# One core, three graph layers: VectorE's small work dealt out to GpSimd and ScalarE, its order changed, and score rows brought by DMA

## What is computed

```python
si = x @ attn_w[l, :d]                      # a number per row
sj = x @ attn_w[l, d:]                      # a number per column
scores = si[:, :, None] + sj[:, None, :] + attn_b[l]
scores = where(scores >= 0, scores, 0.2 * scores)
attn = softmax(where(mask, scores, -inf))
h = layernorm(x + attn @ x, g1[l], beta1[l])
ff = gelu(h @ W1[l] + b1[l]) @ W2[l] + b2[l]      # 256 -> 1024 -> 256
x = layernorm(h + ff, g2[l], beta2[l])
```

## Time and profile before

| | |
|---|---|
| median of 3 runs | 2660.37 us |
| the profiled execution | 2659.89 us, its span 2657.7 us |
| mean granted TensorE clock | 0.976 of full speed |
| PE busy | 2399.8 us, 90% of the span |
| DVE busy | 2365.4 us, 89% |
| ACT busy | 1703.0 us, 64% |
| POOL busy | 517.7 us, 19% |
| DMA queue q1 | 244.39 MB, 32.1% of 16 engines |
| chain that ended last | PE 30%, DVE 23%, ACT 16%, issue 7% |

### The profile page before, as it was taken

The page is one execution under the profiler, slowest core; times in us unless marked ns, Lnnn a source line. Parts: engine busy times, 40 slices in busy tenths (PEclk is TensorE's granted clock), DMA queues, the critical chain, the costliest instruction groups (busy, mean ns, idle before and its releaser), DMA issues.

```text
span 2657.7 us, 45899 instructions
## 1 busy us (share of the span) xinstructions
PE 2399.8 (90%) x16548; PEld 2201.3 (83%) x16548; DVE 2365.4 (89%) x5742; ACT 1703.0 (64%) x2681; POOL 517.7 (19%) x500
## 2 busy tenths in 40 slices
PE   8999999963999999999889999999989999999996
PEld 6999999953888888888788888888878888888886
DVE  5888888878899999999889999999998999999985
ACT  3444444433676776777767776776776677677673
POOL 3555555530000001001010100100000110111111
PEclk9999999986999999999999999999999999999998
DMA  4444444444332322313232232332323234232211
GB/s 148 127 137 141 143 143 135 140 127 109 92 80 64 88 76 76 93 52 88 85 106 58 79 88 72 88 84 60 88 84 103 64 96 108 81 99 81 59 40 40
DMA packets 349875, 247.32 MB, mean 93 GB/s; under 512 B 214480, under 2 KB 308688, under 8 KB 349648
## 3 DMA queue, kind: packets, MB, share of 16 engines
q1 hardware_dynamic: 349648, 244.39, 32.1%
HBM read 143.68 MB, written 50.33 MB: 73 GB/s over the span
## 4 chain that ended last, share of the span: by engine, by line
PE 30%; DVE 23%; ACT 16%; issue 7%; DMA 2%; SPq 1%; ACTq 0%; POOLq 0%; DVEq 0%; POOL 0%
ACT t L964 6%; ACT pT_hi L963 5%; PE Y L1422 5%; PE G L45 4%; PE G L43 4%; PE G L44 4%; PE Y L1424 4%; PE Y L1423 4%; DVE prod L1177 3%; DVE u L1120 3%; DVE xo L1163 3%; DVE xo L1156 2%; ACT L963 2%; DVE spare L1072 2%; DVE st L1124 2%
## 5 line engine op out<-in xcount | busy, mean ns | idle before, releaser
L991 ACT ACTIVATE g<-G,b_less 128x512 f32<-128x512 f32 x384 | 264.0, 688 | 522.5 <-PE G L45 398.3
L1371 PE MATMUL A<-x_hi,pT_hi 128*128 128x258 f32 x1536 | 446.9, 291 | 114.8 <-DVE pT_lo L1108 114.8
L1422 PE MATMUL Y<-w_hi,g_hi 128*128 128x256 f32 x1536 | 441.1, 287 | 77.2 <-DVE g_lo L1206 77.2
L1372 PE MATMUL A<-x_hi,pT_lo 128*128 128x258 f32 x1536 | 437.8, 285 | 0.0
L1373 PE MATMUL A<-x_lo,pT_hi 128*128 128x256 f32 x1536 | 437.1, 285 | 0.0
L1424 PE MATMUL Y<-w_hi,g_lo 128*128 128x256 f32 x1536 | 429.8, 280 | 0.0
L1423 PE MATMUL Y<-w_lo,g_hi 128*128 128x256 f32 x1536 | 429.3, 279 | 0.0
L1371 PEld LDWEIGHTS A<-x_hi,pT_hi 128*128 128x128 f32 x1536 | 295.2, 192 | 125.3 <-issue 112.8
L1422 PEld LDWEIGHTS Y<-w_hi,g_hi 128*128 128x128 f32 x1536 | 289.4, 188 | 105.6 <-DVE g_lo L1206 97.3
L1206 DVE TENSOR_TENSOR g_lo<-g,g_hi 128x512 fp32r<-128x512 f32 x384 | 262.5, 684 | 67.3 <-ACT g_hi L994 65.3
L43 PE MATMUL G<-h_hi,w_hi 128*128 128x512 f32 x768 | 311.2, 405 | 5.7 <-DVE h_lo L1201 5.2
(11 more groups left out here) (176 smaller groups left out, 5857.0 us busy)
## 6 DMA issues: line engine op xcount, KB each, us to landing
mask<-mask SPq DMA_DIRECT2D x192, 256.0 KB, 3.3
a_adj_t<-in_adj SPq DMA_DIRECT2D x64, 512.0 KB, 4.0
x_rows<-rows SPq DMA_DIRECT2D x24, 1024.0 KB, 7.4
mask<-a_mask SPq DMA_DIRECT2D x64, 256.0 KB, 4.3
rows<-xo SPq DMA_DIRECT2D x32, 512.0 KB, 2.9
a_xs<-in_x SPq DMA_DIRECT2D x9, 1024.0 KB, 9.5
x_rows<-in_x SPq DMA_DIRECT2D x8, 1024.0 KB, 7.9
rows<-a_xo SPq DMA_DIRECT2D x64, 128.0 KB, 3.7
```

The costliest lines, as they stand in the source:

```text
L1371: pe.matmul(L.A[:, t, 0:DE], hi, L.x_hi[:, par, j, :], start=(j == 0), stop=False)
L1372: pe.matmul(L.A[:, t, 0:DE], lo, L.x_hi[:, par, j, :], start=False, stop=False)
L1422: pe.matmul(L.Y[:, t, :], hi, L.w2[0][:, f, :], start=False, stop=False)
```

## The change

The two products with `g2` and `beta2` become one DVE instruction each over all four tiles (`scaled`), and the normalisation in front of them goes to ScalarE (`n2`, with scale and bias made on GpSimd). `row_columns`, `v_prepare` and `shift1` go to GpSimd, `row_columns` in two halves. On DVE, `norm1` is cut in two: `sums` comes behind `g_lo(k-1, 0)` and `stats1` behind `g_lo(k-1, 2)`; the projections of one tile each are behind f = 1, 3, 5, 7; three of four `row_top` are ahead of the loop over f and one at f = 5, none at its end; in the last layer the closing sum, statistics and norm are at f = 1, 3 and 6. From the second graph on (n >= 2) `vrow` and `rrow` are no longer made by PE and ScalarE: SP stores the columns to lines in DRAM, four bytes at a time, and loads each line back on all partitions; `vrow` is doubled for it. `rows_made(k)` is graph 2 for k = 0 and graph (k+5)//2 for odd k. `row_columns(n, part)` is seven GpSimd instructions of 128x4; `deviation1` has the same four steps as `deviation2` below; `n2` stands behind `h(k-1)` on ScalarE. At the start, six `row_top` instead of eight come before the first scores.

```diff
+            def store_v(n):
+                slot = NCH * n % C
+                if n >= B:
+                    sp.wait_ge(L.s_uv, 2 * TC * (NCH * n + NCH - C))
+                    ...
+                    for c in range(NCH):
+                        sp.dma_start(vline[n, c * BANK:(c + 1) * BANK].rearrange("(t p) -> p t", p=P),
+                                     L.uv[:, slot + c, 1, :]).then_inc(L.s_vline, 16)
+            def load_v(n):
+                sp.wait_ge(L.s_vline, 32 * (n - 1))
+                sp.wait_ge(L.s_top, NT * (n - 1))
+                sp.dma_start(L.vrow[:, n % 2, :], vline[n].partition_broadcast(P)).then_inc(L.s_vrow_in[n % 2], 16)
+            def store_r(n):
+                sp.wait_ge(L.s_cols, COLS * (n + 1))
+                    ...
+                    for part in range(2):
+                        sp.dma_start(rline[n, part].rearrange("(s p) -> p s", p=P), L.rcol[:, part, :]).then_inc(L.s_rline, 16)
+            def load_r(k):
+                n, cs = k // 2, slice(k % 2 * BANK, (k % 2 + 1) * BANK)
+                sp.wait_ge(L.s_rline, 32 * n)
+                sp.wait_ge(L.s_t, NT * (k - 1))
+                for part in range(2):
+                    sp.dma_start(L.rrow[:, part, k % 2, :], rline[n, part, cs].partition_broadcast(P)).then_inc(L.s_rrow_in[k % 2], 16)
...
+                for n in rows_made(k):
+                    store_v(n)
+                if k % 2 == 1 and k + 2 < K:
+                    load_r(k + 2)
...
                 for r in tops[:1]:
                     load_mask(r + MASKS)
-                if k >= 2:
+                for n in rows_made(k):
+                    load_v(n)
+                if k >= 2 and layer_of(k - 2) < LAYERS - 1:
+                    store(k - 2)
+                if k % 2 == 0 and k + 2 < K:
+                    store_r((k + 2) // 2)
+                    load_r(k + 2)
+                if k >= 2 and layer_of(k - 2) == LAYERS - 1:
                     store(k - 2)
...
+            def row_columns(n, part):
+                done = COLS * n + COLS // NCH * part
+                cs = slice(TC * part, TC * (part + 1))
+                pool.wait_ge(L.s_top, NT * n + TC * (part + 1))
+                ...
+            def deviation2(m):
+                if m >= 1:
+                    pool.wait_ge(L.s_n2, TC * m)
+                pool.wait_ge(L.s_mv2, TC * (m + 1))
+                pool.tensor_tensor(L.ve2[:, :], L.mv2[:, :, 1], L.eps[:, :], ALU.add).then_inc(L.s_rs2, 1)
+                pool.wait_ge(L.s_rs2, 4 * m + 1)
+                pool.tensor_tensor(L.rstd2[:, :], L.ve2[:, :], L.half[:, :], ALU.pow).then_inc(L.s_rs2, 1)
+                pool.tensor_tensor(L.nm2[:, :], L.mv2[:, :, 0], L.minus[:, :], ALU.mult).then_inc(L.s_rs2, 1)
+                pool.wait_ge(L.s_rs2, 4 * m + 3)
+                pool.tensor_tensor(L.nmr2[:, :], L.nm2[:, :], L.rstd2[:, :], ALU.mult).then_inc(L.s_rs2, 1)
             for k in range(K + 2):
                 if k >= 2:
-                    deviation2(L.s_mv2, TC * (k - 1), L.s_rs2, k - 2)
...
+                    deviation2(k - 2)
+                if k % 2 == 0 and (k + 2) // 2 < NB:
+                    for part in range(NCH):
+                        row_columns((k + 2) // 2, part)
+                for n in rows_made(k):
+                    v_prepare(n)
                 if k < K:
                     deviation1(k)
+                if k - 2 >= K - C:
+                    deviation3(k - 2 - (K - C))
...
+            def n2(m):
+                act.wait_ge(L.s_rs2, 4 * (m + 1))
+                if m >= 1:
+                    act.wait_ge(L.s_xst, 16 * m)
+                for t in range(TC):
+                    act.activation(L.xo[:, t, :], L.Y[:, t, :], ACT.Identity, bias=L.nmr2[:, t:t + 1],
+                                   scale=L.rstd2[:, t:t + 1]).then_inc(L.s_n2, 1)
...
             def scaled(m):
+                dve.wait_ge(L.s_n2, TC * (m + 1))
+                ...
+                dve.tensor_tensor(L.xo[:, :, :], L.xo[:, :, :], L.g2[:, :].unsqueeze(1).to_broadcast([P, TC, D]),
+                                  ALU.mult).then_inc(L.s_scaled, 1)
+                dve.wait_ge(L.s_scaled, 2 * m + 1)
+                dve.tensor_tensor(L.xo[:, :, :], L.xo[:, :, :], L.be2[:, :].unsqueeze(1).to_broadcast([P, TC, D]),
+                                  ALU.add).then_inc(L.s_scaled, 1)
...
+                early = 3 if k >= 1 else 1
                 if agg:
                     p_lo(k, LEAD)
                 if old:
                     stats2(k - 2)
                 if agg:
-                    for j in range(LEAD + 1, NT - 1):
+                    for j in range(LEAD + 1, NT):
                         p_lo(k, j)
-                if old:
-                    centred(k - 2)
-                if agg:
-                    p_lo(k, NT - 1)
-                for r in tops[:1]:
+                if k == 0:
+                    for r in range(NT, NT + NT - 1):
+                        row_top(r)
+                for r in tops[:min(early, 2)]:
                     row_top(r)
                 if ffn:
                     h_lo(k - 1)
+                for r in tops[2:early]:
+                    row_top(r)
                 if old:
                     scaled(k - 2)
-                if projected:
-                    projections(k - 2)
-                elif old:
-                    final_stats(k - 2)
                 if ffn and new_layer(k - 1):
                     less_b2(layer_of(k - 1))
-                if agg:
-                    norm1(k)
                 for f in range(KF):
                     if ffn:
                         g_lo(k - 1, f)
-                    ...
+                    if f == 0 and agg:
+                        sums(k)
+                    if f == 2 and agg:
+                        stats1(k)
+                    if f in (1, 3, 5, 7) and projected:
+                        projections(k - 2, (f // 2,))
                     if after:
                         score(k + 1, f)
                         if f >= 1:
                             add_mask(k + 1, f - 1)
+                    if old and not projected:
+                        if f == 1:
+                            final_sum(k - 2)
+                        if f == 3:
+                            final_stats(k - 2)
+                        if f == 6:
+                            final_norm(k - 2)
                     if f in (4, 6) and k + 2 < K:
                         x_lo(k + 2, f // 2 - 2)
-                    if f in (3, 5):
-                        for r in tops[f // 2:f // 2 + 1]:
+                    if f == 5:
+                        for r in tops[early:]:
                             row_top(r)
...
-                for r in tops[3:]:
-                    row_top(r)
...
-                    if f == 1 and k < K:
-                        pe.wait_ge(L.s_u, TC * (k + 1))
-                        if k % 2 == 0 and k + 4 < K:
-                            v_row((k + 4) // 2)
-                    if f == 2 and k + 2 < K:
-                        r_rows(k + 2)
                     if ffn:
                         down(k - 1, f)
```

246 lines of the change are left out of this document (129 added, 117 removed).

## The result

The changed kernel takes 2668.26 us in the median of 20 runs (2662.34 to 2675.57), the kernel before on the same chip 2661.73 us (2656.72 to 2668.60). The ratio is 1.0026, 95% interval 1.0016 to 1.0037: no gain, slower by 0.26%, which is less than the 0.3% that I had taken for no difference. I had predicted 2626 us, 2608 to 2656. Ratios are of fast runs alone, and one of the six executions of c_store (experiment 7) was slow, 12389.69 us, so it is in that kernel's median and not in its ratio.

The account below looks back on a forecast made before the run. It took DVE's list to bound a stage, with PE and ScalarE waiting at two places. The terms -26 + 7 - 18 - 1 + 1 = -37, taken as -34, gave 2626 us from 2659.9, range 2608 to 2656.

Parts of the forecast that it names:

- What bounds the kernel: A stage of 40.60 us is DVE's list, with PE and ScalarE waiting for it at two places.
- The steady stage: Projected stages of layers 1 and 2: 39.65 us in place of 40.60, for 27 stages -26 us.
- The rows by DMA: Transposes leave PE and copies leave ScalarE, nothing on the path; stores and loads of lines hidden, delaying only SP's queue.
- I take 4 us to DRAM ... bounds 2 and 10: Storing the row columns to DRAM: 4 us, and 8 us for the load back, bounds 2 and 10 each.
- First three stages of a layer: Stages of 43.9, 47.6 and 40 or 41.3 us, where they took 46.5, 48.7 and 46.5; together -18 us.
- The start: First p_lo at about the same time: 0, give or take 3 us; the stages of the first chunks gain 1.
- The last layer: Nine stages of 41.0 us, three of 39.8: 488 against 485.7, +3, and 4 more for PE's pauses: +7 us.
- The signs: Prediction wrong if scaled takes over 3 us, g_lo(0) starts behind T + 15.6, or the middle's granted clock falls below 1.00.
- E: Layer starts don't gain, because the weights come late and the waits stay: 2644 us, chance 0.12.
- D: n2, masks or lines come 1 us later than the 2.7 us allow: 2668 us, with half 2647; chance 0.06.
- B: PE's changed pauses lower its clock, 1.7 us per 4 us stretch; one in each of 42 stages gives 2697; chance 0.18.
- C: Four GpSimd steps behind g_lo(0) each hold DVE for 0.2 us, 34 us in all: 2660 us, chance 0.06.

Follow-up runs that it names:

- c_store: a_rows_pe plus the changed kernel's stores of columns to DRAM lines, with nothing that reads them or waits for them in SyncE's queue; 2636.98 us, ratio 0.9905.
- experiment 7: The stores of columns alone, added to a_rows_pe without loads of lines or waits for a landing in SyncE's queue (c_store); 2636.98 us, ratio 0.9905.
- a_rows_pe: The changed kernel with its dealing of DVE and GpSimd work kept, but all rows made by PE transposes and ACT copies again; 2624.35 us, ratio 0.9862.
- a_wide_store: The changed kernel with columns stored as one 16- or 32-byte piece per partition in place of 4-byte pieces; 2626.83 us, ratio 0.9858.
- f_dma_top4: Rows by DMA, first weights ahead of the store, and one row maximum moved from behind gelu 5 to ahead of the first g_lo; 2743.28 us, ratio 1.0312.
- a_load_last: The changed kernel with weight loads issued before the waiting load of row vectors at each layer's first stage; 2644.08 us, ratio 0.9952.

## Why the prediction was wrong, by its own steps

*What bounds the kernel* was read rightly: DVE's list from `g_lo(0)` on, with PE and ACT up to it. Before, the two stretches are 18.54 and 21.66 (22.47 in an even stage); after, 15.3 and 24.25. I had 15.33 and 24.4.

*The steady stage*, 39.65 us: measured 39.54 (timeline of PE below). The gain was 23 us where 26 stood; `scaled` takes 2.5 us (2.4), g_lo(0) starts at T + 15.25 to 15.3 (T + 15.3), PE's waits before `down` 6, 7 and `aggregate` are 1.03, 0.83 and 1.6 us (1.0, 1.1, 1.9), all at a granted clock of 1.00:

```profile
1037.16 0.39 PE L1513 MATMUL Y<-w_hi,g_hi 128*128 128x256 f32 x1 [1.03 <-DVE g_lo L1297]
...
1039.63 0.39 PE L1513 MATMUL Y<-w_hi,g_hi 128*128 128x256 f32 x1 [0.83 <-DVE g_lo L1297]
...
1042.88 0.36 PE L1462 MATMUL A<-x_hi,pT_hi 128*128 128x258 f32 x1 [1.61 <-DVE pT_lo L1210]
```

DVE's wait before `g_lo(0)` is 1.9 us, not 2.7; ahead of it stands `n2`, here on ACT's timeline:

```profile
1012.30 1.94 ACT L1110 ACTIVATE xo<-Y,nmr,rstd 128x256 f32<-128x256 f32 x4 [1.74 <-POOL nmr L1031]
```

It ends at T + 10.9, a microsecond after my upper bound, and still fits. What is late is GpSimd: its four steps take 5.5 us where I had 3.3, at most 4.5, and 3.43 of them is the first, on POOL's timeline:

```profile
1006.81 3.43 POOL L1026 TENSOR_TENSOR ve<-mv,eps 128x4 f32<-128x4 f32 x1 [15.32 <-DVE mv L1244]
```

The 23 us hide a larger gain and a loss. The common stage is 1.06 us shorter than before, 28 us for 27 stages, and a_rows_pe and a_wide_store have it all. The changed kernel gives 5 us back in a few stages: 15, 21 and 31 take 41.1, 41.7 and 40.4 us. In stage 15 two row maxima wait 1.67 and 2.15 us for their masks, which is more than DVE has to spare, and `g_lo(0)` starts at T + 16.9. The second of them:

```profile
1253.86 1.23 DVE L1184 CUSTOM_DVE_ANT_0 spare<-vrow,mask 128x1024 bf16<-128x1024 f32 x1 [2.15 <-DMA mask<-mask]
```

In stages 21 and 31 the first gelu starts late, and the trace does not show why.

*The rows by DMA: "nothing on the path"* was right of PE and ACT and is why that part could bring nothing. Wrong was its price, and this is the step that failed: **"I take 4 us to DRAM ... bounds 2 and 10"**, and with it "the weights come some 8 us later than now, up to 2 us of which I charge". The stores of the two columns land in 11.4 to 12.6 us (14.7 in stage 0), outside my bounds; the load back, with 8 us, was priced too high (3.6 in the median). The nearest row I had, a load of 1024 four-byte values, was one for the other direction. The weights were issued at T + 28.2 where they had been at T + 12.8, 15 us later. And I charged only the one who waits, not that the stores hold up the transfers issued right behind them. The Trainium skill (DMA: Bandwidth & Descriptors) warns of both, and I drew on neither. Its section "Specifications" gives 512 bytes as the least transfer for the full rate, and says that below it the DMA does a read-modify-write. Pieces of 4 and of 32 bytes are both below that, and the store took 11.9 and 1.9 us, so no run here shows that bound or that way of writing. Its section "Queues, rings and completion order" has the increment of a semaphore land only after every earlier write of the same DMA engine. That fits the 11.8 us of the weights behind the store. "The line is needed at T + 55: hidden from any bound" was true of the line and blind to the queue.

*First three stages of a layer*, -18 us forecast: +2.7 and +4.9 measured, 26 off. The third stages did what I said (39.5 and 40.8, where 40 and 41.3 stood; `be2` and the low clock gone), the first two lost what is told above. Not all of the 26 is the price of the stores: in a_wide_store, without that price, the three stages are still 3 and 4 us over my 131.5 and 132.8. The term is the second stage, 50.2 and 51.2 us where I had 47.6 (before: 48.2 and 49.1); the new dealing lengthens it, in a_rows_pe too (50.1 and 52.4), and what sets it stays open. *The start*, 0 give or take 3, and -1 for the first chunks: +17, for the same reason, since stage 0 has stores, weights and masks in one queue; 18 off. *The last layer*, +7: stages 35 to 47 took 489.9 us (488 + 4 forecast) against 485.7. With the end it is +2 where +8 stood. Together 26 + 18 + 3 less 6 is the 40 us, rounded, between -37 and +3.

*Where the forecast and the runs meet.* With the larger pieces the same change measures 2626.83 us, the 2626 that I had forecast. That is in part luck: its steady stages give 28 us (26), its layer starts 11 (18), its last layer and end cost 2.5 (8), and its start costs 4.4 (a gain of 1).

*The signs.* Of the three by which I called the prediction wrong beforehand none came in a common stage: `scaled` takes 2.5 us, `g_lo(0)` starts by T + 15.3 in most stages (at T + 16.9, 17.5 and 16.2 in 15, 21 and 31), and the clock of the middle is 1.00. All three look at the steady stages, and the failure is at the starts: three stages of a layer take 144.5 and 146.3 us where I had said some 131.

*The rivals.* E named the right place and mechanism, with 18 us where 43 were due. D, late data in all stages, has the measured time, 2668 us, but that is chance: masks came late in a few steady stages, which cost less than 5 us together, and the rest is at the starts. B did not occur in the steady stages; in stages 16 and 32 the clock was lower than before, and in f_dma_top4 it fell in steady stages too. C does not show (group of the page, part 5: busy us, mean ns, idle before):

```profile
L1297 DVE TENSOR_TENSOR g_lo<-g,g_hi 128x512 fp32r<-128x512 f32 x384 | 264.5, 689 | 128.9 <-ACT g_hi L1124 122.8
```

689 ns with GpSimd at 983 us of work, 684 with it at 518, and from `g_lo(0)` on DVE is busy 24.20 of 24.24 us in either dealing of the rows. Of the rule on the shared port (the Trainium skill, SBUF — State Buffer, section "SBUF: two separate sides") DVE's side is not seen here. GpSimd's steps are longer, and more than I expected: the first on a mean and variance takes 1961 ns where it took 532 or 469. That would fit its side of the rule, but no run tests it.

## What to carry to other kernels

Price a small transfer by how it is cut into pieces and not by its bytes, and charge it to everything behind it in its queue, not only to its reader. Cut a stage where one engine waits for another, and ask of each saving in which stretch it falls: 1.1 us of PE and 1.6 us of DVE a stage were worth nothing here, and 1.15 us in the right stretch was worth 14 us of time (not more, since the move overfilled the other stretch of every second stage). When a change has two parts, cost each alone: here they removed the same wait, and one of them brought a price.

## What the hardware showed that I had not expected

A store of two columns of 1024 four-byte values (2 x 4 KB) lands after 11.4 to 12.6 us in the changed kernel, and mostly after 1.9 us (3.8 at most) when each partition's eight values go as one piece. Loads issued within 4 us behind it land 10 to 15 us after their issue (weights 10.5 to 10.9 in a_load_last, masks 9.8 to 14.7 in the changed kernel) in place of 2.2 and 4.2.

In the changed kernel the first GpSimd step of a chain takes 1.9 us in the mean:

```profile
L1026 POOL TENSOR_TENSOR ve<-mv,eps 128x4 f32<-128x4 f32 x48 | 94.1, 1961 | 720.4 <-DVE mv L1244 720.4
```

In a_rows_pe the same step takes 0.95 us in the mean (its other chain 1.54), with nothing changed on GpSimd's list there but the copy of a column. What lengthens it is open.
